# Values of the first cross attention: shares as the stationary operand, context rows moving as pairs of halves

## What is computed

```python
q = jnp.einsum('bsh,oh->bso', query, WQ)
k = jnp.einsum('bsh,oh->bso', key, WK)
v = jnp.einsum('bsh,oh->bso', value, WV)
scores = jnp.einsum('bqh,bkh->bqk', q, k) / jnp.sqrt(jnp.float32(hidden_size))
attn = jax.nn.softmax(scores, axis=2)
return jnp.einsum('bqk,bkh->bqh', attn, v)
```

## Time and profile before

| what | value |
|---|---|
| median of 3 runs | 1068.14 us |
| the profiled execution | 1071.49 us |
| its span in the trace | 1069.7 us |
| the stage `context_rows`, in the trace | 224.9 to 336 us |
| TensorE busy, share of the span | 90% |
| VectorE, ScalarE, GpSimd busy | 39%, 29%, 19% |
| granted TensorE clock, mean over the span | 0.941 |

### The profile page before, as it was taken

One profiled execution on the slowest core, in us unless ns is written; L12 is line 12 of the kernel. 1 busy time (PEld: TensorE's weight loads), 2 busy tenths in 40 slices (PEclk: granted clock), 3 DMA queues, 4 the chain that ended last, 5 costly groups with the idle time before them and its releaser, 6 DMA issues. The chain is left out here.

```text
span 1069.7 us, 19297 instructions
## 1 busy us (share of the span) xinstructions
PE 966.8 (90%) x7844; PEld 765.2 (72%) x7844; DVE 413.8 (39%) x946; ACT 306.8 (29%) x822; POOL 201.9 (19%) x285
## 2 busy tenths in 40 slices
PE   4989999989999889999999999998799888999772
PEld 4886665668886344479999999968665477999320
DVE  3683443213332451001212232271267512556565
ACT  3322222132220120122232242222676422221253
POOL 4252000000000224000000010020365203222465
PEclk9999999999999969999999999958899988999895
DMA  9966000154723516259998888210400004670001
GB/s 263 381 226 211 2 2 1 40 194 156 261 112 140 184 30 213 80 218 384 369 357 280 276 278 275 78 51 1 125 24 2 2 1 166 238 262 1 1 16 46
DMA packets 72169, 159.07 MB, mean 149 GB/s; under 512 B 4100, under 2 KB 5653, under 8 KB 70289
## 3 DMA queue, kind: packets, MB, share of 16 engines
q1 hardware_dynamic: 69760, 153.59, 41.6%
q0 software_dynamic: 2320, 4.25, 1.2%
HBM read 125.85 MB, written 31.97 MB: 148 GB/s over the span
## 5 line engine op out<-in xcount | busy, mean ns | idle before, releaser
L1914 PE MATMUL ps<-ffn_h,ffn_w 128*128 128x128 f32 x1280 | 149.0, 275 | 0.0
L1914 PEld LDWEIGHTS ps<-ffn_h,ffn_w 128*128 128x128 f32 x1280 | 145.8, 192 | 0.0
L1914 PE MATMUL ps<-ffn_xh,ffn_w 128*128 128x128 f32 x640 | 74.9, 275 | 0.3 <-ACT ffn_xh L1941 0.3
L1914 PEld LDWEIGHTS ps<-ffn_xh,ffn_w 128*128 128x128 f32 x640 | 73.1, 192 | 0.9 <-issue 0.9
L1992 DVE TENSOR_SCALAR ffn_h<-ps,tile_bias 128x128 f32<-128x128 f32 x80 | 22.5, 344 | 120.6 <-PE ps L1914 120.6
L463 POOL TENSOR_SCALAR rstd<-mean_var 100x1 f32<-100x1 f32 x16 | 6.0, 374 | 229.4 <-DVE mean_var L423 229.4
L1346 PE MATMUL ps<-x_qT,ctx_ct 128*128 128x100 f32 (+1 forms) x384 | 44.8, 279 | 0.0
L2008 DVE SCALAR_TENSOR_TENSOR ffn_y<-ps,tile_bias,ffn_gate_row 128x128 f32<-128x128 f32 x80 | 22.6, 344 | 57.1 <-PE ps L1914 57.1
L1955 ACT ACTIVATE ffn_y<-ffn_y 128x128 f32<-128x128 f32 x80 | 23.8, 298 | 73.0 <-DVE ffn_y L2008 73.0
L2403 POOL TENSOR_TENSOR att_e<-att_e,decay 100x400 f32<-100x400 f32 x32 | 32.7, 1033 | 60.0 <-DVE att_e L2252 60.0
L1346 PEld LDWEIGHTS ps<-x_qT,ctx_ct 128*128 128x128 f32 (+1 forms) x384 | 43.7, 192 | 0.0
(11 more groups left out here) (423 smaller groups left out, 1924.2 us busy)
## 6 DMA issues: line engine op xcount, KB each, us to landing
ffn_w<-in_L_ffn_w_dram SPq DMA_DIRECT2D x60, 1024.0 KB, 6.4
shelf<-in_ctx_dram SPq DMA_DIRECT2D x12, 1280.0 KB
expert_rows<-nothing SPq DMA_DIRECT2D x1, 14820.0 KB, 50.1
context_turned<-ctx_ct SPq DMA_DIRECT2D x8, 1444.0 KB, 11.9
ctx_ct<-context_turned SPq DMA_DIRECT2D x6, 1444.0 KB, 6.1
ctx_lent<-in_ctx_dram SPq DMA_DIRECT2D x4, 1280.0 KB
rows_own<-expert_rows SPq DMA_DIRECT2D x8, 260.0 KB, 3.0
x_wo<-in_L_xattn_Wo_dram SPq DMA_DIRECT2D x1, 2048.0 KB, 7.7
```

The source lines that it names most:

```text
L1914: mm = nc.tensor.matmul(acc(n)[:, m, :], w[:, n % SLOTS, k, m * P:(m + 1) * P], into[l][:, i % 2, k, :], start=k == 0, stop=k == C - 1, sk ...
```

## The change

Only `context_rows` changes. Shares become the stationary operand ([128 keys x 100 tokens]) and the context rows the moving one (512 columns), as three products of halves for each of the 6 tiles. For that:

- ScalarE splits off the high half of each row's context (`split`, L1252, 4 pieces: two of 128x1024, one of 128x512, one of 82x512) into `raw_high`, two buffers; GpSimd subtracts it from the raw row (L1299), in place of the raw row, into `raw_low`. It waits until the row has been turned.
- ScalarE's `keep_p` writes the high half of the turned shares (L1268), VectorE's new `low_of_p` the low half (L1337).
- The output of a row is now tokens by features, [100 x 512]. VectorE copies it (`keep_natural`, L1345) to `an`, TensorE turns it with 4 transposes (`turn_out`, L1172) in the next iteration, through the same ring of 3 banks, and ScalarE copies it to `xf` (`keep_out`, L1243), which VectorE did before.
- The order of the units in the ring is now a list (`order`), with the output of b-1 between tiles 1 and 2 of row b+2.

```diff
             raw = raws
+            raw_low = ([sb_at(f"{name}_low{i}", [P, KT, D], shelf_at + 4 * KT * D * i, FR) for i in range(3)]
+                       + [sb_at(f"{name}_low{3 + i}", [P, KT, D], xT_at + 4 * C * N * i, FR) for i in range(2)])
+            raw_high = [sb(f"{name}_high{i}", [P, KT, D], FR, phase) for i in range(2)]
             ct = [sb(f"{name}_ct{i}", [P, C, S], F32, phase) for i in range(2)]
             pn = sb(name + "_pn", [T, 2, S], F32, phase)
-            pT = sb(name + "_pT", [P, 2, KT, T], F32, phase)
+            pT = Pair(*(sb(f"{name}_pT_{half}", [P, 2, KT, T], FR, phase) for half in ("hi", "lo")))
+            an = sb(name + "_a", [T, 2, D], F32, phase)
...
+            PIECES = ((0, P, 0, 2), (1, P, 2, 4), (2, P, 4, KT - 1), (3, LAST, KT - 1, KT))
+            order = [("t", 0, j) for j in range(KT)] + [("t", 1, j) for j in range(KT)]
+            for b in range(B):
+                order += [("t", b + 2, j) for j in (0, 1) if b + 2 < B]
+                order += [("a", b - 1)] if b else []
+                order += [("t", b + 2, j) for j in range(2, KT) if b + 2 < B]
+            order.append(("a", B - 1))
+            at = {u: n for n, u in enumerate(order)}
+            to_dve = lambda u: u[0] == "t" and u[2] in BY_DVE
+            DVES = [sum(to_dve(u) for u in order[:n + 1]) for n in range(len(order))]
+
...
             def tile_of(b, j):
-                return ps[:, (KT * b + j) % RING, :].rearrange("p (c k) -> p c k", c=C)[:, :, 0:keys(j)]
+                return ps[:, at["t", b, j] % RING, :].rearrange("p (c k) -> p c k", c=C)[:, :, 0:keys(j)]
+
+            def out_of(b):
+                return ps[:, at["a", b] % RING, 0:C * T].rearrange("p (c t) -> p c t", c=C)
...
+                    def turn_out(b):
+                        pe.wait_ge(natural_a, b + 1)
+                        bank_free(("a", b))
+                        for c in range(C):
+                            mm = nc.tensor.transpose(out_of(b)[:, c, :], an[:, b % 2, c * P:(c + 1) * P], ident[0:T, 0:T])
+                        mm.then_inc(turned, 1)
...
-                    def value(b, c):
-                        if c == 0:
-                            pe.wait_ge(kept_p, 2 * (b + 1))
+                    def value(b, js):
+                        if js[0] == 0:
+                            pe.wait_ge(low_p, 2 * (b + 1))
                             if b >= 1:
-                                pe.wait_ge(a_kept, b)
-                        for j in range(KT):
-                            mm = nc.tensor.matmul(ps[:, VB, c * T:(c + 1) * T],
-                                                  raw[b % RAWS][0:keys(j), j, c * P:(c + 1) * P],
-                                                  pT[0:keys(j), b % 2, j, :], start=j == 0, stop=j == KT - 1,
-                                                  skip_group_check=True)
-                        if c == C - 1:
+                                pe.wait_ge(natural_a, b)
+                        for j in js:
+                            pe.wait_ge(low_raw, len(PIECES) * b + (j // 2 + 1 if j < KT - 1 else len(PIECES)))
+                            r = slice(0, keys(j))
+                            products = times(pT[r, b % 2, j, :], Pair(raw_high[b % 2], raw_low[b % RAWS])[r, j, :])
+                            for n, (p_, c_) in enumerate(products):
+                                mm = nc.tensor.matmul(ps[0:T, VB, :], p_, c_, start=j == 0 and n == 0,
+                                                      stop=j == KT - 1 and n == 2)
+                        if js[-1] == KT - 1:
                             mm.then_inc(used, 1)
...
-                        value(b, 0)
+                        if b:
+                            turn_out(b - 1)
+                        value(b, (0, 1))
                         turn(b + 2, (2, 3))
-                        value(b, 1)
+                        value(b, (2, 3))
                         turn(b + 2, (4, 5))
-                        value(b, 2)
-                        value(b, 3)
+                        value(b, (4, 5))
                         if b + 1 < B:
                             turn_p(b + 1)
+                    turn_out(B - 1)
...
+                    def keep_out(b):
+                        act.wait_ge(turned, at["a", b] + 1)
+                        nc.scalar.activation(aT_out[:, :, b * T:(b + 1) * T], out_of(b), ACT.Identity).then_inc(by_act, 1)
+
+                    def split(b, pieces):
+                        if b < B:
+                            for i, rows_, j0, j1 in (PIECES[n] for n in pieces):
+                                if i == 0:
+                                    act.wait_ge(landed[b % RAWS], 32 * (b // RAWS + 1))
+                                    if b >= 2:
+                                        act.wait_ge(used, b - 1)
+                                nc.scalar.activation(raw_high[b % 2][0:rows_, j0:j1, :], raw[b % RAWS][0:rows_, j0:j1, :],
+                                                     ACT.Identity).then_inc(high_raw, 1)
...
+                    keep(0, range(4))
+                    split(0, (0,))
+                    keep(0, range(4, KT))
+                    split(0, (1, 2, 3))
+                    keep(1, (0, 1))
                     expo(0)
-                    high(1, range(2, KT))
+                    keep(1, range(2, KT))
                     keep_p(0)
                     for b in range(B):
-                        high(b + 2, (0, 1))
+                        keep(b + 2, (0, 1))
                         if b + 1 < B:
                             expo(b + 1)
-                        high(b + 2, range(2, KT))
+                        if b:
+                            keep_out(b - 1)
+                        keep(b + 2, (2, 3))
+                        split(b + 1, (0, 1))
+                        keep(b + 2, (4, 5))
+                        split(b + 1, (2, 3))
                         if b + 1 < B:
                             keep_p(b + 1)
+                    keep_out(B - 1)
+
+                @block.gpsimd
+                def _(pool):
+                    for b in range(B):
+                        pool.wait_ge(turned, at["t", b, KT - 1] + 1)
+                        for i, rows_, j0, j1 in PIECES:
+                            pool.wait_ge(high_raw, len(PIECES) * b + i + 1)
+                            nc.gpsimd.tensor_tensor(raw_low[b % RAWS][0:rows_, j0:j1, :], raw[b % RAWS][0:rows_, j0:j1, :],
+                                                    raw_high[b % 2][0:rows_, j0:j1, :].bitcast(F32), ALU.subtract
+                                                    ).then_inc(low_raw, 1)
...
-                    def keep_a(b):
+                    def low_of_p(b):
+                        if b >= 2:
+                            dve.wait_ge(used, b - 1)
+                        for i, rows_, j0, j1 in PARTS:
+                            dve.wait_ge(high_p, 2 * b + i + 1)
+                            nc.vector.tensor_tensor(pT.lo[0:rows_, b % 2, j0:j1, :], ps[0:rows_, 5 + i, 0:(j1 - j0) * T].rearrange(
+                                "p (j t) -> p j t", t=T), pT.hi[0:rows_, b % 2, j0:j1, :].bitcast(F32), ALU.subtract
+                                ).then_inc(low_p, 1)
+
+                    def keep_natural(b):
                         dve.wait_ge(used, b + 1)
-                        nc.vector.tensor_copy(aT_out[:, :, b * T:(b + 1) * T],
-                                              ps[:, VB, 0:C * T].rearrange("p (c t) -> p c t", c=C)).then_inc(a_kept, 1)
-
-                    low(0, range(KT))
+                        if b >= 2:
+                            dve.wait_ge(turned, at["a", b - 2] + 1)
+                        nc.vector.tensor_copy(an[:, b % 2, :], ps[0:T, VB, :]).then_inc(natural_a, 1)
...
-                        keep_a(b)
+                        keep(b + 2, range(2, KT))
+                        keep_natural(b)
+                        if b + 1 < B:
+                            low_of_p(b + 1)
```

More of the change, by code:

```diff
@@ L1090, in context_rows @@
+            an = sb(name + "_a", [T, 2, D], F32, phase)
             st = sb(name + "_st", [T, 2, 4], F32, phase)
             landed = ctx_landed[0]
-            (turned, ct_act, ct_dve, scored, peak, less, ex, root, even, turned_p, kept_p, used, a_kept) = (
-                sem(f"{name}_{s}") for s in (
-                    "turned", "ct_act", "ct_dve", "scored", "peak", "less", "exp", "root", "even", "turned_p", "kept_p",
-                    "used", "a_kept"))
+            (turned, by_act, by_dve, scored, peak, less, ex, root, even, turned_p, high_p, low_p, used, natural_a, high_raw,
+             low_raw) = (sem(f"{name}_{s}") for s in (
+                 "turned", "by_act", "by_dve", "scored", "peak", "less", "exp", "root", "even", "turned_p", "high_p", "low_p",
+                 "used", "natural", "high_raw", "low_raw"))
@@ L1096, in context_rows @@
             stored = [sem(f"{name}_stored{i}") for i in range(2)]
```

(48 more changed lines are left out.)

27 lines of the change are left out of this document (11 added, 16 removed).

## The result

The changed kernel takes 1064.17 us, median of 20 runs (1060.28 to 1066.92), beside 1068.2 us for the kernel before, also 20 runs (1062.69 to 1073.22). The ratio is 0.9959 with a 95% interval of 0.9941 to 0.9976: 4.4 us less (2.6 to 6.3), where the medians alone give 4.0. The forecast was 1064.1. The profiled execution has a span of 1065.1 us, before 1069.7, both at a mean granted clock of 0.941.

A forecast was written before the change was run, and what follows sets the result against it. TensorE, without a gap in a full row, was taken as the bound. Gains 1.17 + 5 x 0.83 = 5.32 less losses 1.1 + 0.2 gave 4.0 us, so 1064.1 us on the median; range 1057 to 1076.

The forecast's parts named there:

- Only TensorE sets the row: Full row of the stage: TensorE has no gap, 13.17 of 13.17 us, so work taken off it shortens the row.
- Values 18 x 0.231 = 4.16: Value products of a row: 18 instructions at 0.231 us each, 4.16 us in place of 5.33.
- Turnings 0.87 + 0.88 + 0.72, and 0.34 for the output: TensorE's transposes in a row: tile turnings at their old prices, plus 4 new output transposes at 0.34 us.
- Row 0 gains 1.17, the start loses 0.2: Start of the stage: row 0 turns no output, 1.17 us less; a split ahead of tile 4 costs 0.2 us.
- ScalarE hidden by a slack of 0.9: Copy of tile 4, for which the scores wait: ready 0.9 us early despite the splits, so no cost.
- GpSimd 2.05 ns a column, 7.2 us a row, hidden: Subtractions for the low half: 3072 columns a row, 7.2 us beside TensorE's 12.3 us, ready 6 us early.
- The end loses 1.1: Last row: waits for the low half and GpSimd, plus output turning; output at T+14.1, before T+13.0, 1.1 us lost.
- Rival 1: Value products: passes set the pace or switching float32/float32r eats the gain; 5.12 us a row, 1070.7 us; chance 0.13.
- Rival 2: GpSimd's subtraction: dearer but hidden, 2.68 ns a column, last row's pieces later, gain 2.3, 1065.8 us; chance 0.15.
- rival 3: TensorE's wait before every tile: GpSimd becomes the bound from about 3.8 ns a column, 4 to 54 us slower; chance 0.09.
- middle case: GpSimd as the bound at 4.7 ns a column: a row takes 15.3 us, the end comes 17 later, 1085 us.
- Rival 4: Value products: the stream runs at the floor of 0.215 us, 0.29 a row more gained, 1062.4 us; chance 0.08.

The follow-up runs named there:

- The one-part experiments: Against the kernel before: float32r halves in the old orientation, 1107.8 us, ratio 1.0367; new orientation with whole float32, 1070.36 us, ratio 1.0008.

## Why the prediction was right, point by point

- **Only TensorE sets the row.** Right: 12.38 of 12.38 us busy, and neither the absence of GpSimd's work nor the earlier splits moves the row by more than 0.01.
- **Values 18 x 0.231 = 4.16.** 4.38 measured, 0.22 more. The pace of 0.23 is right; each portion's first product stands 0.07 further from the second. The price was taken from a stream without changes of kind, so it had no term for this.
- **Turnings 0.87 + 0.88 + 0.72, and 0.34 for the output.** 0.87 + 0.79 + 0.68 and 0.29, 0.18 less. The two errors nearly cancel, and a row of 12.38 instead of 12.34 is what is left. Both stand at the changes from transposes to float32r products; that time only passes from the last transposes to the first product is likely, but no run shows it.
- **Row 0 gains 1.17, the start loses 0.2.** Together 0.97 forecast, 1.46 - 0.17 = 1.29 measured. What failed is the term for the start: the store lands 20.24 us into the stage as before, so all of the later start is absorbed where I had left 0.2 of it. From the store to the row's end it is 10.02 us (244.92 to 254.94) instead of 11.26 (245.19 to 256.45), 1.24 less, near the 1.17.
- **ScalarE hidden by a slack of 0.9.** Right, with 1.3 for 0.9, and the experiment with doubled splits shows the edge where it was put: the copy of tile 4.
- **GpSimd 2.05 ns a column, 7.2 us a row, hidden.** 7.15 measured. The experiment with doubled subtractions shows that it is the bound at 14.9 us a row, as the mechanism said. Hidden holds for the middle rows; the last row pays 0.48.
- **The end loses 1.1.** The mechanism was right, step by step: low half first (a wait of 1.03), then GpSimd. The size was 0.84. The start of values(7) was off by most, T + 7.08 for T + 7.8: ScalarE's four splits took 3.04 us where I added 3.3, and started at T + 2.57, not T + 2.79. But most of these 0.7 us did not reach the output, since the last tile waited for GpSimd all the same: its last piece came at T + 10.97 (327.78) where the sum had 11.2, and that 0.23 is the gain over the forecast.
- **Rival 1, the passes or a switch.** Refuted: values take 4.38 us a row, not 5.12, and a switch costs at most the 0.07 above. The one-part experiments say why. A float32r product with 128 stationary columns costs what a float32 one does, 0.111; one with 512 moving columns costs 0.23, against 0.43 for a float32 instruction.
- **Rival 2, GpSimd at 2.68 ns**, and **rival 3, GpSimd the bound.** No: 2.37 us for 1024 columns. Rival 3 is real only with its work doubled. (Its middle case, 15.3 us a row, adds up to 18 us later by its own rule, not 17.)
- **Rival 4, the floor of 0.215.** The mean within a portion is 0.23.

So the stage gained 4.45 where the sum said 4.0: start and row 0 are better by 0.32, the end by 0.26, five rows worse by 5 x 0.03 = 0.15. That the median came out within 0.1 us of the forecast is luck: the terms were off by up to 0.3 with both signs, and single runs spread over 6.6 us. What the record bears out is the gain, 4.4 (2.6 to 6.3) for 4.0, and where it arises.

## What to carry to other kernels

Before splitting float32 into halves look at how many columns move: with 100 moving and 128 stationary an instruction costs its load, and halves make it 3 instructions for 2; with 512 moving they make 0.69 us out of 0.86. Judge helper engines by the place where the bound engine waits for them, not by their busy share: ScalarE at 54% was 1.3 us from the critical path, GpSimd at 58% some 6 us (its first piece of row b+1 ends at about 274.6, and those values start at 280.87). And what hides in a steady row is bare in the last one, so price the end of a loop by itself, and look there for reordering.

## What was unexpected of the hardware

- **The clock can fall under a full TensorE.** In the kernel with halves in the old orientation the engine was busy for 16.03 of 16.03 us in a stretch whose mean granted clock was 0.80; from 283.6 to 290 it was 0.50, and starts stood 0.21 apart instead of 0.111, so the clock had gone from 2.4 to 1.2 GHz there. TensorE's last wait ahead of it ended at 236.79, 47 us earlier. In the changed kernel the whole stage stays at 1.00. Why these products of 100 columns lose the upper level, no run here shows.
- **GpSimd and VectorE slow each other.** Scaling 100x722 in the on-chip memory takes 0.60 us alone, 0.70 to 2.07 beside GpSimd's subtraction, depending on how they overlap; a 512-column piece of GpSimd goes from 1.27 to up to 1.60, while its pieces of 1024 columns keep their 2.36. Copies out of the product banks (0.69) are unchanged.
- **The first float32r product behind transposes** stands 0.30 us from the second, where the others stand 0.23 apart, and the transposes ahead of it look up to 0.09 cheaper. It is not the transposes alone: 0.30 and 0.31 stand also behind waits for the shares (323.89) and for GpSimd (327.83), and at 325.36, where GpSimd's piece had only just come.
